# The first layer of a four-layer block, chunk by chunk as x arrives

## The reference, cut to what matters

```
def _gn(v, G=32, eps=1e-05):
    g = v.reshape(B_, H_, W_, G, C_ // G)
    m = jnp.mean(g, axis=(1, 2, 4), keepdims=True)
    s = jnp.var(g, axis=(1, 2, 4), keepdims=True)
    return ((g - m) / jnp.sqrt(s + eps)).reshape(v.shape)

A1 = jnp.einsum('noi,bint->bont', P1, A)          # A = _gn(x); n: 32 columns, i, o: 32 rows, t: 64 channels
A3 = jnp.einsum('noi,bin->bon', P3, A.mean(-1))
x = jax.nn.relu(A1 + 0.1 * A3[..., None])
mean = x.mean(axis=(0, 2, 3), keepdims=True)      # per row o, over images, columns and channels
var = x.var(axis=(0, 2, 3), keepdims=True)
x = (x - mean) * jax.lax.rsqrt(var + BN_EPS) * gamma + beta
```

## Time and profile before

| | us |
|---|---|
| median of three executions | 1069.65 |
| lowest and highest | 1063.14, 1072.01 |
| profiled execution, own time | 1064.25 |
| its span, first to last instruction | 1062.3 |
| mean granted TensorE clock, share of full | 0.938 |
| TensorE busy | 872.5 (82%) |
| VectorE (DVE) busy | 736.5 (69%) |
| ScalarE (ACT) busy | 482.6 (45%) |
| GpSimd (POOL) busy | 275.9 (26%) |

### The profile page before, as it was taken

One profiled execution on the slowest core, in us unless ns is written; L12 is line 12 of the kernel. 1 busy time (PEld: TensorE's weight loads), 2 busy tenths in 40 slices (PEclk: granted clock), 3 DMA queues, 4 the chain that ended last, 5 costly groups with the idle time before them and its releaser, 6 DMA issues.

```text
span 1062.3 us, 21730 instructions
## 1 busy us (share of the span) xinstructions
PE 872.5 (82%) x8899; PEld 595.6 (56%) x8899; DVE 736.5 (69%) x949; ACT 482.6 (45%) x594; POOL 275.9 (26%) x198
## 2 busy tenths in 40 slices
PE   0233995187989988998998886999999996999997
PEld 0231443043544444444544455899999995677776
DVE  8999955456676886777777765346666666577776
ACT  1321466386765755565654332222222221555554
POOL 5209802400321222222232220000000000866660
PEclk9996897598999989999999988999999999899999
DMA  9732222222333110101110011133333340011112
GB/s 194 167 40 48 107 99 94 97 108 108 126 122 128 29 24 23 23 23 23 28 41 23 22 32 44 57 119 120 119 119 119 119 149 1 20 60 56 52 59 69
DMA packets 46996, 80.01 MB, mean 75 GB/s; under 512 B 14944, under 2 KB 23264, under 8 KB 45792
## 3 DMA queue, kind: packets, MB, share of 16 engines
q1 hardware_dynamic: 39040, 69.77, 21.0%
q10 hardware_dynamic: 7872, 9.00, 3.8%
HBM read 59.90 MB, written 35.10 MB: 89 GB/s over the span
## 4 chain that ended last, share of the span: by engine, by line
PE 66%; DVE 8%; issue 3%; ACT 3%; POOL 2%; ACTq 0%; DVEq 0%; POOLq 0%
PE ps L1231 63%; PE ps L1577 1%; DVE st L951 1%; PE ps L1569 1%; POOL WK L497 1%; DVE RG L1098 1%; ACT XB L626 1%; ACT WK L632 1%; DVE me L961 1%; DVE WK L1016 1%; PE ps L1304 1%; ACT RG L632 1%; ACTq L698 0%; DVE WK L939 0%; DVE WK L1106 0%
## 5 line engine op out<-in xcount | busy, mean ns | idle before, releaser
L1231 PE MATMUL ps<-WK,RG 64*64 64x224 f32 (+3 forms) x1216 | 244.2, 397 | 22.1 <-DVE RG L880 18.1
L1231 PEld LDWEIGHTS ps<-WK,RG 128*128 128x128 f32 (+1 forms) x1216 | 214.4, 269 | 46.6 <-issue 43.6
L1231 PE MATMUL ps<-WK,WT 64*64 64x512 f32 (+2 forms) x1216 | 188.7, 636 | 15.1 <-DVE WK L1016 6.6
L1231 PE MATMUL ps<-RG,WT 64*64 64x512 f32 (+1 forms) x832 | 140.8, 629 | 20.8 <-POOL TMP L537 14.7
L632 ACT ACTIVATE WK<-ps,BC 128x1024 f32<-128x1024 f32 x96 | 105.7, 1113 | 95.8 <-PE ps L1231 88.3
L742 ACT ACTIVATE WK<-ps 128x1024 f32<-128x1024 f32 x48 | 49.1, 1024 | 164.8 <-PE ps L1231 164.8
L1231 PEld LDWEIGHTS ps<-WK,WT 64*64 64x64 f32 (+1 forms) x1216 | 56.7, 144 | 110.7 <-issue 80.7
L632 ACT ACTIVATE RG<-ps,BC 128x1024 f32<-128x1024 f32 x96 | 105.5, 1113 | 28.9 <-PE ps L1231 25.8
L561 POOL TENSOR_TENSOR RG<-WK,gates 128x512 f32 (+1 forms) x32 | 42.4, 1323 | 247.4 <-ACT WK L750 238.3
L1231 PEld LDWEIGHTS ps<-WK 32*32 32x32 f32 x4096 | 64.1, 145 | 41.4 <-issue 41.2
L1231 PE MATMUL ps<-WK 32*32 32x32 f32 x4096 | 69.6, 226 | 12.7 <-issue 12.5
(11 more groups left out here) (185 smaller groups left out, 1443.6 us busy)
## 6 DMA issues: line engine op xcount, KB each, us to landing
band_rows<-band_tables SPq DMA_DIRECT2D x64, 192.0 KB
band_rows<-band_tables SPq DMA_DIRECT2D x32, 384.0 KB
RG<-band_rows SPq DMA_DIRECT2D x16, 768.0 KB, 4.2
RG<-band_rows SPq DMA_DIRECT2D x8, 1536.0 KB, 6.4
WK<-WK ACTq DMA_DIRECT2D x64, 136.0 KB
XB<-in_x_dram SPq DMA_DIRECT2D x32, 256.0 KB, 8.4
out_dram<-WK SPq DMA_DIRECT2D x64, 128.0 KB, 2.1
band_tables<-WK SPq DMA_DIRECT2D x8, 94.5 KB
```

Source lines behind the costliest of these rows:

```text
L1231: return nc.tensor.matmul(out, lhsT, rhs, start=start, stop=stop)
```

## The change

The group sums are taken on TensorE: `SHARE`, a column block of 32 equal numbers, is the stationary operand, and the eight columns of a chunk stream through four column tiles of 128 rows by 32 columns. DVE adds channel pairs, TensorE adds the partitions, DVE and ACT (a square root) make the factors of this chunk, all on every partition at once. The mean is no longer subtracted from x: `A` is x times the factor, and the mean's part, together with the A3 term, is a product with few rows. `row_factors` makes these rows' coefficients in 24 products of 32 columns, ACT copies them, and `add_rows` adds them with eight products of 32 rows each. Every chunk goes from load to relu before the next. The loads of P1 and P3 go from SP to ACT's queue. The band tables never lie in SBUF: SP clears them in DRAM from a tile of zeros and writes the taps from DRAM to DRAM. The batch norm's chain on DVE comes behind the preparation of later weights, and TensorE's wait for `spread_set` goes from tick 0 to the first use of `SPREAD`.

```
@@ sync: x first, P loads gone, then the weights, then the tables @@
-                if ch == NCH // 2:
-                    sp.wait_ge(sem("zeroed"), 5)
...
-                if ch == NCH - 2:
-                    store_bands(0)
-            store_bands(1)
+            sp.wait_ge(sem("zeroed"), 4)
...
+            for l in range(LEVELS):
+                for w in range(W4):
+                    sp.dma_start(band_dram.ap()[l, :, w, 0:TABLE[l]].rearrange("p (m n) -> p m n", n=378),
+                                 zeros.to_broadcast([NU, TABLE[l] // 378, 378])).then_inc(sem("band_zeroed"), 16)
+            sp.wait_ge(sem("band_zeroed"), 16 * LEVELS * W4)
...
+                            sp.dma_start(dst, src).then_inc(sem("band_set"), 16)
+            sp.wait_ge(sem("band_set"), 16 * taps)
@@ gpsimd @@
-            for l in range(LEVELS):
-                nc.gpsimd.memset(BAND_SB[l], 0.0).then_inc(sem("band_zero"), 1)
...
-                nc.gpsimd.tensor_tensor(A(XCH * ch, XCH), XA[:, b], m_b, ALU.subtract).then_inc(sem("centred"), 1)
@@ scalar @@
+            squares(0)
+            deviations(0)
             act.wait_ge(sem("pt_mm"), 1)
...
+            squares(1)
+            for ch in range(NCH):
+                if ch + 1 < NCH:
+                    deviations(ch + 1)
+                row_factors(ch)
+                if ch + 2 < NCH:
+                    squares(ch + 2)
+                relu(ch)
@@ vector @@
+            for ch in range(NCH):
+                TT(a, XA[:, b], R64[ch % 2]..., ALU.mult).then_inc(sem("a_ready"), 1)
+                if ch + 1 < NCH:
+                    pairs(ch + 1)
+                nc.vector.tensor_reduce(SUMA[ch % 2]..., a, AX.X, ALU.add).then_inc(sem("suma_ready"), 1)
+                if ch + 1 < NCH:
+                    variances(ch + 1)
+                    factors(ch + 1)
+            def variances(ch):
+                link(TS(MEAN0, e[:, 0, :], -1.0, None, ALU.mult))
+                link(TT(VAR0, MEAN0, MEAN0, ALU.mult))
+                link(TT(VAR0, e[:, 1, :], VAR0, ALU.subtract))
+                TS(VAR0, VAR0, 0.0, EPS_GN, ALU.max, ALU.add).then_inc(sem("var0_ready"), 1)
+            def factors(ch):
+                link(nc.vector.reciprocal(r, SD0...))
+                link(TT(RBT[ch % 2]..., MEAN0..., r, ALU.mult))
+                link(nc.vector.tensor_reduce(MEANS[ch % 2][:, 0:XCH], RBT[ch % 2]..., AX.X, ALU.add))
+                STT(RBT[ch % 2], RBT[ch % 2], mean_row, BATCH1, ALU.mult, ALU.add).then_inc(sem("rows_ready"), 1)
@@ tensor @@
+            def sums0(ch):
+                    for e in range(2):
+                        for j in range(W4):
+                            last = mm(ps[32 * j:32 * (j + 1), ch % 2, 256 * i:256 * (i + 1)], SHARE, v[:, :, 2 * j + e, :],
+                                      e == 0, e == 1)
+            def row_factors(ch):
+                for e in range(2):
+                    for j in range(W4):
+                        mm(o, SUMA[ch % 2][:, 32 * k:32 * (k + 1)], P3T[:, k, :], True, False)
+                        mm(o, MEANS[ch % 2], P3T[:, k, :], False, False)
+                        last = mm(o, PLUS, P1T[:, k, :], False, True)
+            def add_rows(ch):
+                for e in range(2):
+                    for j in range(W4):
+                        last = mm(ps[:, 4 + j, 256 * e:256 * (e + 1)], CT0[ch % 2][p, P * e:P * (e + 1)], RBT[ch % 2][p, :],
+                                  False, e == 1)
+            for ch in range(NCH):
+                layer0(ch, 0)
+                if ch + 1 < NCH:
+                    means0(ch + 1)
+                layer0(ch, 1)
+                row_factors(ch)
+                add_rows(ch)
+                if ch + 2 < NCH:
+                    sums0(ch + 2)
...
@@ tensor, before tick 0 and in spread(s) @@
-            pe.wait_ge(sem("spread_set"), 4)
+                if s == 0:
+                    pe.wait_ge(sem("spread_set"), 4)
```

More of the change, by code:

```diff
@@ L584, in _, with squares @@
+            for w4 in range(W4):
+                p = slice(H * w4, H * (w4 + 1))
+                act.dma_start(P1N[p, :, H * w4:H * (w4 + 1)],
+                              P1[WB * w4:WB * (w4 + 1), :, :].rearrange("k o i -> o k i")).then_inc(sem("p_loaded"), 16)
+                act.dma_start(P3N[p, :, H * w4:H * (w4 + 1)],
+                              P3[WB * w4:WB * (w4 + 1), :, :].rearrange("k o i -> o k i")).then_inc(sem("p_loaded"), 16)
+            def squares(ch):
                 act.wait_ge(sem(f"x_loaded{ch}"), 16 * W4)
@@ new lines, in row_factors, with relu @@
+            def row_factors(ch):
+                act.wait_ge(sem("ct_mm"), ch + 1)
+                nc.scalar.activation(CT0[ch % 2], ps[:, 2 + ch % 2, 256:512], ACT.Copy).then_inc(sem("ct_ready"), 1)
+            def relu(ch):
+                for u in range(2):
+                    n = 2 * ch + u
+                    act.wait_ge(sem("relu_mm"), n + 1)
+                    r0 = A(XCH * ch, XCH, slice(4 * u, 4 * (u + 1))).rearrange("p b k c -> p k b c")
+                    o = unit(2 + u).rearrange("p (k b c) -> p k b c", k=4, b=XCH)
+                    nc.scalar.activation(r0, o, ACT.Relu, accum_out=xs[:, 0, n:n + 1]).then_inc(sem("relu_done"), 1)
+                    act.wait_ge(sem("relu_done"), n + 1)
+                    nc.scalar.activation(o, r0, ACT.Square, accum_out=xs[:, 1, n:n + 1]).then_inc(sem("relu_sq"), 1)
@@ L813, in _ @@
             nc.vector.memset(epsm[:, 1:2], EPS_GN / P).then_inc(sem("epsm_set"), 1)
-            link(nc.vector.memset(sums[:, :, :, :], 0.0))
+            nc.vector.memset(SHARE, 1.0 / (32 * 2 * TOK)).then_inc(sem("ones_set"), 1)
+            nc.vector.memset(sums[:, :, :, :], 0.0).then_inc(sem("sums_zero"), 1)
+            link(nc.vector.memset(PLUS, 0.0))
+            nc.vector.memset(PLUS[:, XCH:XCH + 1], 1.0).then_inc(sem("ones_set"), 1)
+            for i in range(2):
+                link(nc.vector.memset(SUMA[i], 0.0))
+                link(nc.vector.memset(MEANS[i], 0.0))
             link(nc.vector.memset(meanm[:, :], 0.0))
@@ new lines, in means0, with layer0 @@
+            def means0(ch):
+                pe.wait_ge(sem("pairs_ready"), ch + 1)
+                mm(ps[:, 2 + ch % 2, 0:256], ones[:, :], PAIRS[ch % 2]).then_inc(sem("mean0_mm"), 1)
+            def layer0(ch, u):
+                pe.wait_ge(sem("a_ready"), ch + 1)
+                if ch >= 1:
+                    pe.wait_ge(sem("relu_sq"), 2 * ch - 1 + u)
+                for k in range(4 * u, 4 * (u + 1)):
+                    mm(ps[:, 4 + k // 2, 256 * (k % 2):256 * (k % 2 + 1)], P1T[:, k, :], A(XCH * ch, XCH, k), k % 2 == 0, False)
@@ new lines, in _ @@
+            pe.wait_ge(sem("ones_set"), 4)
+            sums0(0)
+            means0(0)
+            pe.wait_ge(sem("ident_set"), 1)
+            pe.wait_ge(sem("p_loaded"), 16 * 2 * W4)
+            for k in range(WB):
+                nc.tensor.transpose(unit(2)[:, P * k:P * (k + 1)], P1N[:, k, :], ident[:, :])
+                last = nc.tensor.transpose(unit(3)[:, P * k:P * (k + 1)], P3N[:, k, :], ident[:, :])
+            last.then_inc(sem("pt_mm"), 1)
+            sums0(1)
+            pe.wait_ge(sem("pt_ready"), 2)
```

291 lines of the change are left out of this document (108 added, 183 removed).

## The result

| | before | after |
|---|---|---|
| median, us (runs) | 1068.05 (4) | 1011.38 (4) |
| lowest to highest, us | 1063.14 to 1072.01 | 1007.65 to 1016.16 |
| ratio, 95% interval | | 0.9482, 0.944 to 0.9523 |
| profiled execution, us (span) | 1064.25 (1062.3) | 1013.91 (1011.7) |
| last accumulator read of the layer ends, us | 167.57 | 129.93 |

The forecast was 1016 with 998 to 1040. Between the profiled executions the gain is 50.3 us, which is also the sum of the prediction. The terms of that sum were not all right, though, and the experiments show which ones cancelled. Ratios of the experiments are against runs of the kernel before that were taken together with them; slow executions are left out of the ratios, so a ratio can differ a little from the quotient of two medians.

The account below looks back on a forecast made before the run. No engine is full in the first layer, so the path through the engines bounds it. Gains of 41.0 (layer), 1.8 and 7.5 (behind it) sum to 50.3 off 1064.25: 1014, as median 1016, range 998 to 1040.

Parts of the forecast that it names:

- A: Row factors and sums on TensorE: only two of four tiles run at a time, round 12.6 us, total 1027; chance 0.18.
- B: TensorE's column tiles run in turn: round 19.8 us without a TensorE gap, total 1075, slower; chance 0.06.
- sign of a wrong forecast: In the layer: TensorE has no gap, or a round is bound by DVE.
- Rival D: Layer's gain taken back by ticks or POOL, or clock stays at 1.2 GHz: gain 10 to 20, total 1048; chance 0.06.
- The landing of P: Layer start: P1 and P3, on ACT's queue, come last, between 10 and 33 us; 22 taken.
- the 27.2 us: From P's landing to the end of chunk 0's relu, TensorE at 1.2 GHz; relu ends near 49.5.
- The round: One chunk of the layer: path from one relu's end through products, row factors, copy, squares and relu, 11.2 us, five times.
- The reciprocal: DVE's reciprocal of 256 columns in each round: between 0.4 and 1.6 us, middle 1.0 taken.
- The last round: Last two rounds of the layer: no squares, added rows show instead, 10.5 us each; relu ends at 126.5.
- Behind the layer: After ACT's batch norm starts: 1.8 us from DVE's order, 9.7 from the `spread_set` wait less 2.2 given back, so 7.5.
- Band tables: SP's row transfers start near 160, rows there near 410, needed about 600: cover 190 us, cost nothing.
- Rival C: P lands near 12 us, DVE and TensorE run ahead, round 10.3, end 15 us earlier, total 1001; chance 0.12.

Follow-up runs that it names:

- the one-line edit: Changed kernel, with SP waiting after chunk 0 of x until P1 and P3 have landed: 994.87 us, ratio 0.9326 to the kernel before.

## Why the prediction was right, and where it was not

**The mechanism held.** Four tiles of 32 columns run at once (0.89 us for eight products), so rivals A and B fall (B's round adds up to 19.7 and not 19.8, which changes nothing). The Trainium skill (TensorE: Matmul & The Clock Gate, Part 3) has weight loads overlap running products only where the row group differs, and the prediction read B from it. The same section also gives a measured speedup of 2.38 for three column tiles, which that reading left out. In this trace all four tiles use all 128 rows and overlap. Roots between squares and relu load no table: two loads of 1283 ns at the layer's start, none more in eight chunks. The Trainium skill (ScalarE: Activation LUTs, Table sets) advises to batch functions by set, and says that relu and copy are in every set; here square and root alternate with them too, as if all four were in one. TensorE has gaps in every round (1.06 and 0.47), DVE waits in it too (0.54, 0.38, 0.81), so neither sign of a wrong forecast is there. Rival D falls as well: the granted clock is 1.00 through the rounds, and what is gained at the first dense product, 48.8 us, is still there at the end.

**The landing of P: 26.4, forecast 22.** The 7.7 to 15.7 us that the forecast started from were P1's loads alone; P3's took 6.5 to 15.0, which moves nothing. The 4.4 us were lost, and 3.8 of them won back, mostly by TensorE's clock: the 27.2 us that I counted from there to the end of chunk 0's relu at 1.2 GHz took 23.4, since the row at 38.88 already shows 1.89 for a half of the layer and not 3.45. Chunk 0's relu ended at 49.87 (49.5). Two errors, one result.

**The round: 11.21, forecast 11.2.** Also by cancelling. The row factors took 2.58 with their tail against 1.6: tiles not in turn, as its experiment shows. From chunk 0's last relu at 49.87 the rows give: second half of the products 2.04 with the 0.19 until it starts (1.8, and part of the 0.3 for shapes), row factors 2.6, copy 0.28 (0.6), squares 1.81 (1.9), relu with squares 4.47 (4.6), and nothing for stretches at 1.2 GHz (0.4; the granted clock is 1.00 from 45 to 111 us). The path itself was in part luck too. TensorE reaches the second half at 50.06 without a wait, straight from the first half, which the square behind the previous chunk's first relu releases at 47.83. So the path that the profile follows back runs over the first relu: TensorE 6.67 us from 47.83 to the end of the row factors, then the copy, the squares ahead, the first relu and its square, 11.2 in all. The prediction's path, over the second relu, is as long within 0.2 us. Round less waits, TensorE was engaged 9.7 us and not 8.6, ACT 6.9 and not 7.2, DVE with its small gaps 9.5 and not 8.7.

**The reciprocal: 1.75, bounds 0.4 to 1.6.** The middle was taken between two readings of a row with eight columns; the price goes by columns, as the upper reading said: 194 ns for 8, 0.95 us for 128, 1.75 for 256. It cost nothing here because DVE had room in the round.

**The last round: 13.27, forecast 10.5.** 2.5 of it is the clock, which I had placed in the rounds before and not behind the longer gap of the last one; the round before it, from relu to relu, took 10.75. The layer ended at 129.93 and not at 126.5; the gain was 37.6 and not 41.0, and the batch norm's chain took 3.23 and not 2.97.

**Behind the layer: 11.4, forecast 9.3.** The experiments separate it: 1.80 from the order of chain and weight preparation (forecast 1.8), 9.7 from the wait (forecast 9.7 less 2.2). The 2.2 that POOL's residuals were to take back are not lost at the first dense product, which the same DVE operation releases in every run that has the wait moved. Some of the 9.7 fades in the next ticks, by how much the runs leave open.

**Band tables: nothing, forecast nothing.** The transfers began at 136.5 and not at 160: 156 issues ahead of them went faster than the 0.9 us that I took. The cover was 214 us (forecast 190), and 130 us taken away left the time as it was.

So 3.6 us too little came from the layer and its chain and 2.1 too much from behind it: 48.8 at the first dense product, and 50.3 at the end. The exact match with the sum is luck of the size of an execution's spread: the same program a second time took 998.68.

**Rival C** (P early) is what the one-line edit made real in its first half: the start comes 14.7 us earlier, and the time is 994.87 us. Its second half, a round of 10.3 because DVE and TensorE run ahead, did not come: the round stays 11.2 (ACT's copies at 28.60 and, six rounds on, at 95.84).

## What to carry to other kernels

Loads that many small transfers make up, and that the first product waits for, go ahead of a large stream and not beside it on another queue: one wait on the issuing queue was worth 13 to 17 us here by the ratios and 14.7 in the trace, beside 57 for the whole change. Small products on tiles of the array should go round the tiles, term by term, not tile by tile. When an edit shortens the busiest engine's work in a loop, look first for the closed path through the engines: shortening the work of DVE, which looked full, left the round at 9.72, while two reorderings on the path through TensorE and ACT had taken 1.5 us off it.

## What the runs showed of the hardware

- Four tiles of 128 rows by 32 columns run at once: eight float32 products of 256 columns in 0.89 us. The same tiles with three products in a row on each took 2.58 us for 24 products of 128 columns, in turn 1.52.
- DVE's reciprocal goes by columns at about 6.3 ns each (0.95 us for 128, 1.75 for 256), where a copy or product of 256 columns takes 0.29 to 0.43.
- Eight loads of 32 KB on ACT's queue took 7.3 to 18.4 us beside 32 of 256 KB on SP's, and 3.7 to 5.6 behind the first four of them.
- After the same gap of 2.47 us TensorE went on at 1.2 GHz in one execution (6.67 us for 16 instructions) and at 2.4 GHz in another of the same program (1.97 for each eight).
